# The first cross sequence's query and key projections, its split tile and its score stacks made in the last pair of the self-attention

## The chip, the core and the metric

The kernel runs on one core of one Trainium2 chip. The metric is the device time of one execution in microseconds (us), the median of three runs. The page and the trace of the profile come from one further execution.

## What is computed

A decoder layer on x of 16 sequences x 256 positions x 512 (float32), in three parts, each added to its input:

```python
x = x + attn(layernorm(x), w_q, w_kv, w_dense)      # causal, 16 heads of 128, 4 groups of keys and values
x = x + xattn(layernorm(x), ctx, mask, mask, Wq, bq, Wk, bk, Wv, bv)
x = x + ffn(layernorm(x), ...)                       # 8 experts, 2 chosen per token

# xattn takes the 256 positions as channels and the 512 columns as time; 16 heads of 16 channels
q = einsum('oc,bct->bot', Wq, target) + bq
k = einsum('oc,bcs->bos', Wk, source) + bk
v = einsum('oc,bcs->bos', Wv, source) + bv
dot = einsum('bhdt,bhds->bhts', q, k) / 4            # masked, softmax over s
out = einsum('bhts,bhds->bhdt', softmax(dot), v)
```

Float32 products are made of float32r parts: each operand is split into a high part (a rounded copy, on ScalarE) and a low part (the difference, on VectorE or GpSimd), and three matmuls (high x high, high x low, low x high) make one product.

## The kernel before, in words

The program is a chain of blocks (`nc.Block`). Each block holds one instruction stream for SyncE (SP), GpSimd (POOL), ScalarE (ACT), VectorE (DVE) and TensorE (PE), written out by hand; the order in a stream is the order in the code, and streams meet only at semaphores. At the end of a block all five meet at a barrier, so the next block starts when the last of the five has reached its end.

**The self-attention block** (`attention_phase`) goes over 8 pairs of sequences (512 tokens) twice, once for each half of the heads: `body(t, kind, half)`, with `kind` "plain", "turn", "fresh" or, for the last pair of the second half, "last". A pair has 16 units `u` (a head and a sequence): scores on PE, the row maximum on DVE, the exponential on ACT, the scaling on DVE and POOL, transposes on PE, their high and low parts on ACT and DVE (`pT`), the product with the values into `ps_c`, and its high and low parts (`cT`). From unit 12 on come the `dense` products; the last four of them (`dense(t, 1, n)`) stand after the units, behind `values_product(t, NH - 1)`. In all pairs but the last, the key, value and query projections of the next pair stand among these; in the last pair nothing does. SP loads and stores at fixed places; in the last pair its last commands are four stores of the finished rows (L258), one for each dense sum.

**The preparation of the cross-attention** (`cross_preparation`) hands small steps to these streams: the three cross weights are split in units 1 to 6 (`weight_high` on ACT, `weight_low` on DVE, each for a whole weight: four instructions for k and for q, one for v); `first_stats` on DVE in unit 5; `norm_scale_of_cross` on POOL; `first_normalised`, `first_x_high`, `first_context_high` on ACT in units 8, 10 and 14; `lows_of_cross` (both low parts) on POOL after the last unit.

**The cross-attention block** (`cross_attention_phase`) goes over 16 sequences `b` of 4 quads `q` of 4 turns `k`. A stack holds, for one quad, the split queries and keys and the mask rows. "M" scores (`max_scores`, L1871) give the row maxima (`maximum`, L1687, on DVE), which go through `split_maxima`, a transpose, `negmax_rows` on ACT (L1533) and two DMAs (`stack_negmax`, L1236) into the stack; "E" scores (`exp_scores`, L1882) then go to the exponential on ACT (L1538). The M scores run two quads ahead, so a prologue comes before `body(0, ...)`: the projections `k0, k1, q0, q1, v0, v1` of sequence 0 (`piece`, L1799), their bias and mask on DVE (`raw_tile`, `raw_values`), the split tile (`tile_high_part` on ACT, `tile_low_part` on POOL), 18 stack DMAs (`stack_half`, L1190: 15 on SP, 3 on POOL), the M scores of quads 0 and 1, and, for sequence 1, its load, `normalise(1)`, `norm_scale(1)`, `context_low(1)`, `normalised(1)`, `x_high(1)` and the projection `k0`.

## Time and profile before

| | us |
|---|---|
| runs | 2795.73, 2787.54, 2796.38; median 2795.73 |
| the profiled execution | 2785.0, its span 2783.5, mean granted TensorE clock 0.975 |
| TensorE busy | 2608.0 (94% of the span) |
| VectorE, ScalarE, GpSimd busy | 1865.9, 1456.0, 1000.9 |
| self-attention block | to 1382.2 |
| cross-attention block | from 1382.6; first E scores at 1419.99, last ones at 2300.8 |
| experts | from about 2407 |

A share of busy time over the span says little here, since the change touches one seam in a span of 2783.5 us: the last pair of the self-attention and the 37 us between the barrier and the first E scores. The trace is read there.

### The profile page before, as it was taken

The numbers are of one execution on the slowest core, as the hardware profiler recorded it, in microseconds if no ns is written. First come the engines' busy times: TensorE is split into PE (matmuls) and PEld (weight loads), VectorE is DVE, ScalarE is ACT, GpSimd is POOL, SyncE is SP. The second block draws the span as 40 slices with busy tenths as digits, with TensorE's granted clock in tenths as the row PEclk, the third lists the DMA queues.
The fourth block names the chain that finished last, engine by engine and source line by source line (L and its number), as shares of the span: only waits on it lengthen the run. The fifth ranks groups of instructions, "written<-read, shape, count | busy, mean of one in ns | idle before, by whom it ended". The sixth has DMA issues, their size and how long they took to land. (4 is left out here: it accounts for less than half of the span.)

```text
span 2783.5 us, 51139 instructions
## 1 busy us (share of the span) xinstructions
PE 2608.0 (94%) x15536; PEld 1814.1 (65%) x15537; DVE 1865.9 (67%) x3829; ACT 1456.0 (52%) x2868; POOL 1000.9 (36%) x1194
## 2 busy tenths in 40 slices
PE   7999999999999999999879999999999986399997
PEld 6888888888788888888734444444444323277775
DVE  6556655566544555544588889899888776577665
ACT  4334433344433344333357777777777675355554
POOL 2112211122211122111346656656665647433332
PEclk9999999999999999999989999999999998799998
DMA  4102222013212011102155556555555558655554
GB/s 151 68 8 75 75 75 75 14 61 137 85 50 76 32 60 60 60 30 79 35 115 126 133 131 141 131 137 136 132 127 137 128 152 283 234 105 107 106 106 84
DMA packets 144961, 282.49 MB, mean 101 GB/s; under 512 B 44016, under 2 KB 46960, under 8 KB 139760
## 3 DMA queue, kind: packets, MB, share of 16 engines
q1 hardware_dynamic: 116944, 214.99, 26.5%
q0 software_dynamic: 23664, 58.09, 10.1%
q10 hardware_dynamic: 4272, 8.40, 1.0%
q8 instruction: 43, 0.70, 0.1%
q14 instruction: 38, 0.31, 0.0%
HBM read 147.82 MB, written 81.68 MB: 82 GB/s over the span
## 5 line engine op out<-in xcount | busy, mean ns | idle before, releaser
L1687 DVE TENSOR_REDUCE b_negmax<-b_ps_s 128x2 f32<-128x1024 f32 x512 | 611.5, 1218 | 62.7 <-PE b_ps_s L1871 56.0
L293 POOL TENSOR_SCALAR probs<-probs,rinv 128x256 f32<-128x256 f32 x256 | 241.7, 944 | 1086.3 <-DVE rinv L468 1086.2
L1538 ACT ACTIVATE b_probs<-b_ps_s 128x1024 f32<-128x1024 f32 x512 | 520.1, 1020 | 197.7 <-PE b_ps_s L1882 196.7
L334 ACT ACTIVATE probs<-ps_s,negmax 128x128 f32<-128x128 f32 x256 | 94.1, 367 | 483.2 <-DVE negmax L461 483.2
L1895 PE MATMUL b_ps_o<-b_probs,b_v_stack 128*32 128x256 f32 (+1 forms) x2816 | 297.0, 494 | 0.9 <-ACT b_probs L1538 0.7
L1882 PEld LDWEIGHTS b_ps_s<-b_stack 56*128 56x128 f32 x1024 | 96.3, 184 | 273.2 <-issue 165.1
L1882 PE MATMUL b_ps_s<-b_stack 56*128 56x512 f32 x1024 | 258.3, 501 | 13.4 <-DVE b_negmax L1687 7.4
L1871 PE MATMUL b_ps_s<-b_stack 54*128 54x512 f32 x1024 | 229.7, 445 | 34.0 <-DMA b_stack<-b_split 16.9
L582 PE MATMUL ps_proj<-xT_h,wq_h 128*128 128x512 f32 x512 | 216.6, 423 | 0.0
L2581 POOL DMA_INDIRECT out<-e_y,e_place_int x71 | 119.2, 1678 | 251.7 <-DMA out<-e_y,e_place_int 215.6
L582 PE MATMUL ps_proj<-xT_l,wq_h 128*128 128x512 f32 x512 | 201.4, 393 | 0.0
L582 PE MATMUL ps_proj<-xT_h,wq_l 128*128 128x512 f32 x512 | 200.9, 392 | 0.0
L468 DVE RECIPROCAL rinv<-rowsum 128x2 f32<-128x2 f32 x256 | 42.3, 165 | 218.8 <-ACT probs L336 218.8
L582 PE MATMUL ps_d<-wd_h,cT_h 128*128 128x512 f32 x384 | 158.0, 412 | 1.4 <-DVE cT_l L417 1.4
L582 PE MATMUL ps_s<-kT_h,qT_h 128*128 128x128 f32 (+1 forms) x512 | 156.7, 306 | 0.0
L1871 PEld LDWEIGHTS b_ps_s<-b_stack 54*128 54x128 f32 x1024 | 100.0, 191 | 82.4 <-ACT b_probs L1538 44.5
L582 PE MATMUL ps_d<-wd_h,cT_l 128*128 128x512 f32 x384 | 150.8, 393 | 0.0
L582 PE MATMUL ps_d<-wd_l,cT_h 128*128 128x512 f32 x384 | 149.6, 390 | 0.0
L329 ACT ACTIVATE pT_h<-ps_pT 128x384 fp32r<-128x384 f32 x256 | 127.0, 496 | 30.8 <-PE ps_pT L658 30.8
L582 PE MATMUL ps_s<-kT_l,qT_h 128*128 128x128 f32 (+1 forms) x512 | 142.8, 279 | 0.0
L417 DVE TENSOR_TENSOR pT_l<-ps_pT,pT_h 128x384 fp32r<-128x384 f32 x256 | 140.6, 549 | 3.2 <-ACT pT_h L329 3.2
L582 PE MATMUL ps_s<-kT_h,qT_l 128*128 128x128 f32 (+1 forms) x512 | 142.1, 277 | 0.0
(344 smaller groups left out, 6628.0 us busy)
## 6 DMA issues: line engine op xcount, KB each, us to landing
b_stack<-b_split SPq DMA_DIRECT2D x336, 128.0 KB
e_row<-rows_by_expert SPq DMA_DIRECT2D x71, 258.0 KB, 2.9
b_out_tiles<-row_sum_inverses SPq DMA_DIRECT2D x64, 256.0 KB
x<-acc SPq DMA_DIRECT2D x15, 1024.0 KB, 4.7
x_in<-in_x SPq DMA_DIRECT2D x8, 1024.0 KB, 8.3
normalised_x_split<-xT_h SPq DMA_DIRECT2D x8, 1024.0 KB, 9.9
normalised_x_split<-xT_l SPq DMA_DIRECT2D x8, 1024.0 KB, 11.1
acc<-in_x SPq DMA_DIRECT2D x8, 1024.0 KB, 11.4
```

The lines of the kernel that those rows point to most:

```text
L293: nc.gpsimd.tensor_scalar(probs[:, s, P:3 * P], probs[:, s, P:3 * P], rinv[:, s, 1:2], None, ALU.mult).then_inc(probs_done, 1)
L329: nc.scalar.activation(pT[0][:, u % 4, :], ps_pT[u % 2][:, 0:3 * P], ACT.Copy).then_inc(pT_high, 1)
L334: nc.scalar.activation(probs[:, s, 0:P], ps_s[s][:, 0:P], ACT.Exp, bias=negmax[:, s, 0:1], accum_out=rowsum[:, s, 0:1])
L417: return nc.vector.tensor_tensor(dst, ps, h.bitcast(F32), ALU.subtract)
L468: nc.vector.reciprocal(rinv[:, s, :], rowsum[:, s, :]).then_inc(rinv_done, 1)
L582: ins = nc.tensor.matmul(out, w[a][w_at], m[b][m_at], start=st, stop=en)
L1538: nc.scalar.activation(probs[:, k % 2, p, :, :], ps[:], ACT.Exp, scale=0.25).then_inc(e_done, 1)
L1687: nc.vector.tensor_reduce(negmax[:, k, p, :], ps[:], AX.X, ALU.max, negate=True).then_inc(m_reduced, 1)
L1871: ins = nc.tensor.matmul(ps[:, i, :], stack[rows, quad, 0, p, k * P:(k + 1) * P], stack[rows, quad, 1, p, :], start=True, stop=True)
L1882: ins = nc.tensor.matmul(ps[:, i, :], stack[rows, q, 1, p, k * P:(k + 1) * P], stack[rows, q, 0, p, :], start=True, stop=True)
L1895: ins = nc.tensor.matmul(ps_o[32 * h:32 * h + 32, cols], v_stack[:, k, HQ * q + h, :], probs[:, k % 2, h // 2, h % 2, cols], start=(k == 0 ...
L2581: nc.gpsimd.indirect_dma_start(out, bass.IndirectOffsetOnAxis(place_int[i][:], 0), y[i][:], None, compute_op=ALU.add).then_inc(y_out[i], 16)
```

## The change

In the last pair, `weight_high` and `weight_low` now do one quarter of k or q (or all of v) in each of units 0 to 8 (ACT) and 1 to 9 (DVE). `first_stats` is at units 2 and 3, `norm_scale_of_cross` at unit 5, `first_normalised` at 9 and 10, `first_x_high` at 11, `first_context_high` at 12, the low part of the context in two halves at 13 and 14 (POOL). PE makes the key projections of sequence 0 between the last transposes and the last `values_product`, and the query projections between that and the first of the last four `dense`, in the banks `ps_proj`. DVE, ACT and POOL make the raw tile and the split tile there; SP issues the mask rows, the load of sequence 1 and 15 stack DMAs, and POOL 3, before the block ends. The stack, the raw tiles and the first split tile get addresses that are free there. The cross block's prologue then holds no k or q projection and no tile; the value projections stand behind the third M score, in other banks.

```diff
@@ attention_phase, sync
                 def body(t, kind, half):
-                    if kind == "fresh":
-                        load_weights_of_cross()
...
                     sp.dma_start(acc[:], tokens(rows, t - half * PAIRS)).then_inc(acc_loaded, 16)
+                    if kind == "fresh":
+                        load_weights_of_cross()
...
+                    if kind == "last":
+                        sp.wait_ge(proj_filled, FILLS * (t + 1))
+                        stack_mask_rows()
+                        load_second_sequence()
+                        stack_first_tile()
                     if kind != "last":
@@ gpsimd
-                        if kind == "last" and u == TB + 2:
+                        if kind == "last" and u == TB + 1:
                             norm_scale_of_cross()
+                        if kind == "last" and u in (UNITS - 3, UNITS - 2):
+                            first_context_low(u - (UNITS - 3))
                     if kind == "last":
-                        pool.wait_ge(proj_filled, FILLS * (t + 1))
-                        lows_of_cross()
+                        first_x_low()
+                        first_tile_low()
@@ scalar
-                        if last and u in (1, 3, 5):
-                            weight_high("kqv"[u // 2])
-                        if last and u == 8:
-                            first_normalised()
-                        if last and u == 10:
+                        if last and u < 9:
+                            weight_high("kqv"[u // 4], u % 4)
+                        if last and u in (9, 10):
+                            first_normalised(u - 9)
+                        if last and u == 11:
                             first_x_high()
-                        if last and u == UNITS - 2:
+                        if last and u == UNITS - 4:
                             act.wait_ge(proj_filled, FILLS * (t + 1))
                             first_context_high()
                     probs_transposed(t, UNITS - 1)
+                    if last:
+                        for p in range(2):
+                            first_tile_high("k", p)
...
                     context(t, NH - 1)
+                    if last:
+                        for p in range(2):
+                            first_tile_high("q", p)
@@ vector
-                        if last and u in (2, 4, 6):
-                            weight_low("kqv"[u // 2 - 1])
-                        if last and u == 5:
-                            first_stats()
+                        if last and 1 <= u < 10:
+                            weight_low("kqv"[(u - 1) // 4], (u - 1) % 4)
+                        if last and u in (2, 3):
+                            first_stats(u - 2)
...
+                    if last:
+                        for p in range(2):
+                            first_raw_tile("k", p)
                     c_low_part(t, NH - 1)
+                    if last:
+                        for p in range(2):
+                            first_raw_tile("q", p)
@@ tensor
+                    if last:
+                        pe.wait_ge(proj_low, FILLS * (t + 1))
+                        for p in range(2):
+                            first_projection("k", p)
                     values_product(t, NH - 1)
+                    if last:
+                        for p in range(2):
+                            first_projection("q", p)
@@ cross_preparation
+        def load_second_sequence():
+            sp.wait_ge(ready["xs_low"], 1)
+            sp.wait_ge(ready["cs_low"], 1)
+            sp.dma_start(x_in[:], x1_seq[1].rearrange("(k p) t -> p k t", p=P)).then_inc(xc_loaded, 16)
+            sp.dma_start(c_in[:], context_seq[1].rearrange("(k p) t -> p k t", p=P)).then_inc(xc_loaded, 16)
+
+        def stack_first_tile():
+            sp.wait_ge(ready["tile_low"], 4)
+            for q in range(QUADS - 1):
+                for i in range(2):
+                    if (q, i) != (0, 1):
+                        stack_half(sp, q, i, ready["stacked"][q])
...
+        def first_stats(k):
+            if k == 0:
+                dve.wait_ge(xc_loaded, 32)
+            nc.vector.bn_stats(stats[:, k, :], x_in[:, k, :]).then_inc(ready["stats_done"], 1)
...
+        def first_projection(n, p):
+            src = xs if n == "q" else cs
+            if p == 0:
+                pe.wait_ge(w_low, W_PARTS[n] + 3)
+                pe.wait_ge(ready["xs_low"] if n == "q" else ready["cs_low"], 1)
+            if n == "q":
+                pe.wait_ge(ready["raw_done"], p + 1)
             for k in range(CT):
+                for a, c in ((0, 0), (0, 1), (1, 0)):
+                    ins = nc.tensor.matmul(banks[p], w[n][a][:, k, p * P:(p + 1) * P], src[c][:, k, :],
+                                           start=(k == 0 and a == 0 and c == 0), stop=(k == CT - 1 and a == 1))
+            ins.then_inc(ready["proj_filled"], 1)
@@ cross_attention_phase, gpsimd
-                for name in TILES:
-                    tile_low_part(0, 0, name)
-                pool.wait_ge(tile_low, 4)
-                stack_half(0, 0, 1, nc.gpsimd)
                 nc.gpsimd.memset(x_res, 0.0).then_inc(xres_clear, 1)
-                pool.wait_ge(xres_clear, 1)
-                load_res(0)
+                context_low(1)
                 for q in range(3):
                     values(0, q)
                 norm_scale(1)
-                context_low(1)
+                pool.wait_ge(xres_clear, 1)
+                load_res(0)
                 x_low(1)
@@ scalar
-                for name in TILES:
-                    tile_high_part(0, 0, name)
                 context_high(1)
                 normalised(1)
                 x_high(1)
                 negmax_rows(None, 0, 0)
@@ tensor
-                for name in TILES + VALUES:
-                    pe.wait_ge(w_low, W_PARTS[name[0]])
-                    piece(None, 0, name, 0)
-                pe.wait_ge(raw_done, len(TILES))
-                pe.wait_ge(vbias_done, len(VALUES))
                 for k in range(TBL):
                     for p in range(2):
                         max_scores("prologue", None, -1, 2, k, p)
+                        if (k, p) == (1, 0):
+                            pe.wait_ge(w_low, W_PARTS["v"])
+                            for name in VALUES:
+                                piece(None, 0, name, 0)
```

**SP at the end of the self-attention block.** The instructions of SP from the load of the sums' input (`acc`) to the first ones behind the barrier. Before:

```order
L243 DMA acc<-x 128x4x512 [waits b_x1_stored,a_consts]
L258 DMA x<-acc 128x512 [waits a_d_added] x4
L206 UNCONDITIONAL_BRANCH
L1208 UNCONDITIONAL_BRANCH [waits barrier_Pool_Activation_PE_DVE_SP_release]
L1230 DMA b_stack<-mask_rows_split 8x2048 [waits b_aux_stored]
L1230 DMA b_stack<-mask_rows_split 8x2048 x5
```

And of the changed kernel:

```order
L241 DMA acc<-x 128x4x512 [waits b_x1_stored,a_consts]
L880 DMA p_stack<-mask_rows_split 8x2048 [waits a_proj_filled]
L880 DMA p_stack<-mask_rows_split 8x2048 x5
L885 DMA p_x_in<-x 128x2x512 [waits b_cs_low,b_xs_low]
L886 DMA p_c_in<-in_context 128x2x512
L844 DMA p_stack<-p_split 16x2x1024 [waits b_tile_low]
L844 DMA p_stack<-p_split 16x2x1024 x14
L263 DMA x<-acc 128x512 [waits a_d_added] x4
L206 UNCONDITIONAL_BRANCH
L1304 UNCONDITIONAL_BRANCH [waits barrier_Pool_Activation_PE_DVE_SP_release]
```

23 DMA commands now stand between the load of `acc` and the four stores of the finished rows, and the barrier behind the stores.

**DVE in unit 2 of the last pair**, from the reciprocal of that unit to the row maxima of unit 3. Before:

```order
L468 RECIPROCAL rinv<-rowsum 128x2 [waits a_exp_done]
L470 TENSOR_SCALAR probs<-probs,rinv 128x128 [waits a_rinv_done]
L417 TENSOR_TENSOR pT_l<-ps_pT,pT_h 128x384 [waits a_pT_high]
L954 TENSOR_TENSOR p_wk_l<-p_w_stage,p_wk_h 128x4x32 [waits b_w_high]
L954 TENSOR_TENSOR p_wk_l<-p_w_stage,p_wk_h 128x4x32 x3
L460 TENSOR_REDUCE negmax<-ps_s 128x1 [waits a_s_filled]
```

In the changed kernel:

```order
L481 RECIPROCAL rinv<-rowsum 128x2 [waits a_exp_done]
L483 TENSOR_SCALAR probs<-probs,rinv 128x128 [waits a_rinv_done]
L430 TENSOR_TENSOR pT_l<-ps_pT,pT_h 128x384 [waits a_pT_high]
L1029 TENSOR_TENSOR p_wk_l<-p_w_stage,p_wk_h 128x4x32 [waits b_w_high]
L1037 BN_STATS p_stats<-p_x_in 128x6 [waits b_xc_loaded]
L473 TENSOR_REDUCE negmax<-ps_s 128x1 [waits a_s_filled]
```

One quarter of `wk` is left here (the first stands in unit 1), and the first statistics, which wait for the loads of `x_in` and `c_in`, moved forward from unit 5.

**ACT behind the barrier.** Before:

```order
L1525 ACTIVATE b_split<-b_raw_k 128x512 [waits b_raw_done] x2
L1525 ACTIVATE b_split<-b_raw_q 128x512 [waits b_raw_done] x2
L1501 ACTIVATE p_c_h<-p_c_in 128x1024 [waits b_vbias_done,b_xc_loaded]
L1511 ACTIVATE p_xn<-p_x_in,p_shift,p_rstd 128x512 [waits b_xs_low,b_scale_done]
L1511 ACTIVATE p_xn<-p_x_in,p_shift,p_rstd 128x512
L1516 ACTIVATE p_x_h<-p_xn 128x1024 [waits b_xn_done]
L1533 ACTIVATE b_nm_rows<-b_ps_p 8x512 [waits b_proj_filled]
```

In the changed kernel:

```order
L1580 ACTIVATE p_c_h<-p_c_in 128x1024 [waits b_vbias_done,b_xc_loaded]
L1590 ACTIVATE p_xn<-p_x_in,p_shift,p_rstd 128x512 [waits b_xs_low,b_scale_done]
L1590 ACTIVATE p_xn<-p_x_in,p_shift,p_rstd 128x512
L1595 ACTIVATE p_x_h<-p_xn 128x1024 [waits b_xn_done]
L1612 ACTIVATE b_nm_rows<-b_ps_p 8x512 [waits b_proj_filled]
```

The four instructions of the split tile are gone from here; the row of maxima (`b_nm_rows`) still stands behind the three steps of sequence 1.

**DVE behind the barrier.** Before:

```order
L1677 TENSOR_TENSOR b_v_raw<-b_ps_s,p_bias_v 128x512 [waits b_proj_filled,b_bias_v_loaded]
L1677 TENSOR_TENSOR b_v_raw<-b_ps_s,p_bias_v 128x512 [waits b_proj_filled]
L1656 BN_STATS p_stats<-p_x_in 128x6 [waits b_xc_loaded]
L1656 BN_STATS p_stats<-p_x_in 128x6
L1659 BN_AGGR p_mv<-p_stats 128x2 [waits b_stats_done,b_w_low]
L1659 BN_AGGR p_mv<-p_stats 128x2
L1687 TENSOR_REDUCE b_negmax<-b_ps_s 128x2 [waits b_m_filled] x8
```

In the changed kernel:

```order
L1764 TENSOR_REDUCE b_negmax<-b_ps_s 128x2 [waits b_m_filled] x4
L1754 TENSOR_TENSOR b_v_raw<-b_ps_p,p_bias_v 128x512 [waits b_proj_filled,b_bias_v_loaded]
L1754 TENSOR_TENSOR b_v_raw<-b_ps_o,p_bias_v 128x512 [waits b_proj_filled]
L1764 TENSOR_REDUCE b_negmax<-b_ps_s 128x2 [waits b_m_filled] x2
L1733 BN_STATS p_stats<-p_x_in 128x6 [waits b_xc_loaded]
L1733 BN_STATS p_stats<-p_x_in 128x6
```

Four maxima stand ahead of the raw values now, and six ahead of the statistics of sequence 1.

## Rows read from the trace of the kernel before

**Rows 1.** Window: its length, busy PE, PEld, DVE, ACT, POOL, PE clock, DMA share.

```profile
1408.00:1420.00 12.00, 9.30 (x28) 4.47 (x28) 11.20 (x12) 0.59 (x1) 3.20 (x5) 0.51 0.50 93
```

**Rows 2.** Timeline of PE at the seam: start, duration, line, tiles, idle before.

```profile
1367.18 0.50 PE L582 MATMUL ps_c<-pT_h,v_h 128*128 128x512 f32 x1 [1.17 <-DVE pT_l L417]
...
1369.91 0.50 PE L582 MATMUL ps_d<-wd_h,cT_h 128*128 128x512 f32 x1 [1.41 <-DVE cT_l L417]
...
1382.78 0.47 PE L1799 MATMUL b_ps_p<-p_c_h,p_wk_h 128*128 128x512 f32 x1 [1.69 <-PEq L206]
...
1388.36 0.28 PE L1799 MATMUL b_ps_s<-p_wv_h,p_c_h 128*128 128x256 f32 x1
...
1398.27 1.65 PE L1871 MATMUL b_ps_s<-b_stack 54*128 54x512 f32 x6 [6.91 <-DMA b_stack<-b_split]
...
1417.18 0.79 PE L1799 MATMUL b_ps_p<-p_c_h,p_wk_h 128*128 128x512 f32 x1
...
1419.99 0.50 PE L1882 MATMUL b_ps_s<-b_stack 56*128 56x512 f32 x2
```

**Rows 3.** Timeline of DVE in a plain pair.

```profile
1225.67 0.69 DVE L486 TENSOR_TENSOR acc<-ps_c,acc 128x512 f32<-128x512 f32 x1 [2.03 <-PE ps_c L582]
...
1264.63 0.69 DVE L486 TENSOR_TENSOR acc<-ps_d,acc 128x512 f32<-128x512 f32 x1
```

**Rows 4.** Timeline of DVE in the last pair and behind it.

```profile
1308.35 0.69 DVE L486 TENSOR_TENSOR acc<-ps_c,acc 128x512 f32<-128x512 f32 x1 [2.03 <-PE ps_c L582]
...
1316.16 1.26 DVE L954 TENSOR_TENSOR p_wk_l<-p_w_stage,p_wk_h 128x128 fp32r<-128x128 f32 x4
...
1351.96 0.69 DVE L486 TENSOR_TENSOR acc<-ps_d,acc 128x512 f32<-128x512 f32 x1
...
1381.13 0.69 DVE L486 TENSOR_TENSOR acc<-ps_c,acc 128x512 f32<-128x512 f32 x1 [2.03 <-PE ps_c L582]
...
1390.05 0.69 DVE L1677 TENSOR_TENSOR b_v_raw<-b_ps_s,p_bias_v 128x512 f32<-128x512 f32 x1 [0.73 <-PE b_ps_s L1799]
...
1393.48 1.28 DVE L1656 BATCH_NORM_STATS2 p_stats<-p_x_in 128x6 f32<-128x512 f32 x2 [1.40 <-DMA p_c_in<-in_context]
...
1399.10 9.14 DVE L1687 TENSOR_REDUCE b_negmax<-b_ps_s 128x2 f32<-128x1024 f32 x8 [3.98 <-PE b_ps_s L1871]
1408.27 1.29 DVE L1692 CAST b_nm_split<-b_negmax 128x16 fp32r<-128x16 f32 x1
```

**Rows 5.** Timeline of SP: issues of DMAs (start, time to issue, count).

```profile
1311.91 0.50 SPq L831 DMA_DIRECT2D p_c_in<-in_context  x1
...
1373.69 8.49 SPq L258 DMA_DIRECT2D x<-acc  x4
...
1391.42 6.08 SPq L1190 DMA_DIRECT2D b_stack<-b_split  x9
...
1411.71 1.45 SPq L1236 DMA_DIRECT2D b_stack<-b_nm_rows  x2
```

**Rows 6.** Timeline of POOL.

```profile
1315.63 0.95 POOL L293 TENSOR_SCALAR probs<-probs,rinv 128x256 f32<-128x256 f32 x1 [2.21 <-DVE rinv L468]
...
1397.68 4.99 POOL L1400 TENSOR_SCALAR b_v_stack<-b_v_raw,p_mask_col 128x64 f32<-128x64 f32 x12
...
1404.43 2.35 POOL L1380 TENSOR_TENSOR p_c_l<-p_c_in,p_c_h 128x1024 fp32r<-128x1024 f32 x1
```

**Rows 7.** Timeline of ACT.

```profile
1404.50 1.52 ACT L1511 ACTIVATE p_xn<-p_x_in,p_shift,p_rstd 128x512 f32<-128x512 f32 x2 [9.96 <-POOL p_shift L1376]
1406.05 1.06 ACT L1516 ACTIVATE p_x_h<-p_xn 128x1024 fp32r<-128x1024 f32 x1
1411.06 0.59 ACT L1533 ACTIVATE b_nm_rows<-b_ps_p 8x512 f32<-8x512 f32 x1 [3.95 <-PE b_ps_p L1846]
```

**Rows 8.** DMAs issued between 1309 and 1325: KB each, us to landing.

```profile
p_c_in<-in_context SPq DMA_DIRECT2D x1, 512.0 KB, 5.8
```

**Rows 9.** The stack DMAs (line L1190) of the whole trace.

```profile
L1190 SPq DMA_DIRECT2D b_stack<-b_split x336: 573/597/2775, 1391.4 to 2241.6; - x168
...
DMA to landing us min/median/max: 3.2/3.7/5.8
```

189 lines of the change are left out of this document (102 added, 87 removed).

## The prediction

> **What bounds the kernel at this seam.** I read the timeline of each engine around the change first, then the windows. Behind the barrier TensorE makes the projections of sequence 0 from 1382.78, is done at 1391.36, and sits idle 6.91 us until the stacks land at 1398.27 [rows 2]. From there on VectorE paces: eight maxima take 9.14 us, 1.14 each, and a split of the maxima follows [rows 4]. The sixteenth is followed by the first E scores at 1419.99 [rows 2]. From the barrier (PE at 1382.78) to them are 37.2 us. I take what comes after to be bound as before, so that an earlier start of the E scores is an earlier end.
>
> In the last pair itself VectorE paces too. In a plain pair the time from its last sum (1225.67) to the next pair's first (1264.63) is 38.96 us [rows 3]; in the last pair 43.61 us (1308.35 to 1351.96) [rows 4]. The 4.65 us more are about what the split weights and the statistics cost VectorE: four quarters take 1.26 us, the statistics 1.28, and v's part, 512 columns, about the 0.69 of its neighbours [rows 4]: with k and q 4.5. And the block ends with SP: its last store waits for the sum that starts at 1381.13 and ends at 1381.82 [rows 4], is issued at 1382.18 (1373.69 + 8.49) [rows 5], and PE starts 0.60 later [rows 2].
>
> **The change, part by part.** The sum goes from the end of the block to the first E scores.
>
> *The weight pieces.* The same instructions stand one to a unit in place of four in a row. If VectorE paces, a quarter costs its 0.3 us wherever it stands: 0. The bounds are a gain of 4.65 (all hidden) and the rival below. I take 0, since the extra time of the pair equals the work.
>
> *The first statistics.* They stand in unit 2 now and wait for both loads. The command for `c_in` is issued at 1311.91 [rows 5] and lands 5.8 us later [rows 8], at 1317.7. VectorE would come there at about 1316.75: in the trace of before its quarters start at 1316.16 at the same place of the stream [rows 4], plus two quarters (one of unit 1, one of unit 2). It stands still for 1.0 us, and what stands behind it (the maxima of unit 3, and with them scores, exponentials, transposes) is late by that: **+1.0**. Bounds 0 and 2, as the landing is counted from the issue's start or its end and by the semaphore.
>
> *The projections in the tail.* 24 matmuls of 512 columns took from 1382.78 to 1388.36, 5.58 us [rows 2]. The key half covers TensorE's idle 1.17, the query half its idle 1.41 [rows 2]; their operands are ready, as POOL makes the context's low part in units 13 and 14 and the input's right behind unit 15, in 2.35 us [rows 6], and the query half starts only at about 1369.6. Dense starts **2.45** us later by following the instructions one by one (5.58 less 2.58 is 3.0; the restart behind an idle stretch, 0.1 slower each time, and the finer spacing give back the rest). Bounds 2.4 and 4.
>
> *SP.* The low tile ends some 6 us behind the start of the query projections: the last quarter is filled at 1372.5; VectorE takes 0.7 for 512 columns [rows 4], ACT 0.6 [rows 7], POOL 1.2 (half of 2.35 [rows 6]), and semaphores lie between, so 1375.7, or 1376.7 with the statistics' 1.0. Then 15 stack commands at 0.676 (9 in 6.08 [rows 5]) are 9.8 to 10.1 us: 1386.6. Only then come the four stores, whose sums are all done by then (the last at 1381.82 + 1.0 + 2.45 = 1385.3), at 0.45 each (a load of `c_in` took 0.50 [rows 5]): 1388.4. With the 0.60 to PE the block gives way at **1389.0**, 6.2 later than before, of which 1.0 and 2.45 are above and **2.8** is SP's queue. Bounds 0 (the stores keep pace) and 5 (each command at 1.0).
>
> *The prologue.* Stacks for quad 0 were issued from 1376.7 on and land after 3.2 to 5.8 us [rows 9], long before 1389.0, so the 6.91 us are gone, and the projections' 8.6 too. But a chain that was hidden before has less cover. With S = 1389.0: VectorE starts its maxima at S + 0.8 (1399.10 against 1398.27); the value projections stand in front of the fourth M score, 24 matmuls of 256 columns, 2.8 us (from 1388.36 to the idle at 1391.36 [rows 2]), and cost it 0.7; the fourth maximum ends at S + 6.0, the two raw values (0.69 [rows 4]) at S + 7.3. ACT's high part of the context, 1.06 for 1024 columns [rows 7], waits for them: S + 8.5. POOL's low part, 2.35: S + 10.9; its twelve products for the values, 4.99 [rows 6]: S + 15.9; the scale and shift, 1.8 (its products end at 1402.67 and ACT starts at 1404.50 [rows 6, 7]): S + 17.7. ACT then does 1.52 + 1.06 and only after them the row of maxima, 0.59 [rows 7]: S + 20.9, though TensorE has transposed them by about S + 14. SP takes 1.45 to issue [rows 5]: S + 22.3. Landing: no row shows that DMA's; it lies between 0 and the 5.8 of the stack DMAs [rows 9], and I take 3. The first E scores then start at **S + 25.3 = 1414.3**. VectorE would allow S + 22 (0.8 + 16 x 1.14, 0.7 idle, 1.3 raw values, 1.5 statistics, a split of 0.2 to 1.3 [rows 4], less the last maximum). So the gain to there is 1420.0 - 1414.3 = **5.7 us**; bounds 1 and 9 by the landing and SP.
>
> *The clock.* In the 12 us ahead of the E scores TensorE had 0.51 of its clock, the lower of 1.2 and 2.4 GHz, at 9.30 us busy [rows 1], and it rose as the E scores began, since the projection `k0` from 1417.18 to 1419.99 [rows 2] kept it busy right up to them. Now there is a hole of 1 to 3 us between that projection and the E scores, so the body likely begins at 1.2 GHz for a few us. Such a stretch doubles matmul time (`k0` took 2.81 for its six matmuls, where 5.58 for 24 behind the barrier make 1.40 for six [rows 2]); I take 3 us of it, of which half shows: **-1.5**. Bounds 0 and 3.
>
> Sum: 5.7 - 1.5 = 4.2 us less, of the profiled execution's 2785.0: 2780.8. That execution was 10.7 below the median of the runs (2795.73), and one run of three lay near it. Against the median: **2791.5**.
>
> **The rivals.** A measurement of this kernel tells about 0.3%, 8.4 us, from no change.
>
> *A. Everything is hidden (faster).* If the maxima's rows land in 1 us, SP keeps up (2 back), TensorE enters and stays at 2.4 GHz, and the pieces hide part of their time behind VectorE's waits for each exponential, the gain is 5.7 + 2 + 2 + 1 or more: 11, 2784.7. Against it: VectorE's stream is strictly in order, and a piece behind `pT_l` cannot fill a wait that stands behind the next maxima. Chance 0.18.
>
> *B. SP becomes the bound of the seam (slower).* The median issue of a stack command is 597 ns, but the longest took 2775 [rows 9]. The stores and the barrier stand behind all fifteen. From 1.0 us each on (5 more) the gain is gone; at 1.6 each, 14 us more, the kernel ends 10 later: 2805. For it: the longest ones stand where other transfers were in flight, as the 1 MB load of sequence 1 is here. Against it: nine in a row kept 0.676 [rows 5]. Chance 0.06.
>
> *C. VectorE waits for POOL at each piece (slower than forecast, within 0.3%).* Each piece reads two SBUF tiles while POOL scales probabilities. Here the row shows pieces from 1316.16 to 1317.42 beside POOL's 1315.63 to 1316.58 [rows 4, 6], four in 1.26, with no wait to be seen. The cast at 1408.27 took 1.29 us for 16 columns while POOL subtracted [rows 4], so there is such a wait for another form. Were it so for the pieces, nine times up to 0.4 us would be 3.6 more, 2795.1. Chance 0.10, inside "same".
>
> The Trainium skill, SBUF — State Buffer, "Who interferes with whom", says that a VectorE instruction with two SBUF inputs contends with GpSimd reads and that whoever comes second is blocked until the first has finished. By that rule C would hold; the cast's row agrees with an exclusive wait, the row of the pieces does not.
>
> *D. The block-local cost outweighs (same).* The clock stays at 1.2 GHz from the start of the prologue: the value projections take 5.6 in place of 2.8, everything behind them comes 3 later: 2794.5. Chance 0.2, inside "same".
>
> **How the numbers follow.** The forecast (gain 1 to 8 us) has 0.46, D 0.2, C 0.1, A 0.18, B 0.06. Of these the forecast, C and D are within 0.3%, A faster, B slower; for the spread of the runs (2787.54 to 2796.38) I move 0.04 from same to slower: faster 0.20, same 0.69, slower 0.11. The likeliest case alone spans 2784 to 2795; with A and the runs' lower level, range 2779 to 2799.
>
> **What the changed profile would show.** A DVE idle of 1 us before the first statistics in unit 2; the interval 43.61 at 44.6; dense in the tail 2.45 later against the last add of the units; SP's four stores in one run right behind fifteen stack commands, and the barrier behind them; no wait for a stack in the prologue; ACT's `b_nm_rows` about 4 us or more behind its transposes, and the first E scores waiting for its DMA, 25 us behind the barrier in place of 37; a clock of 0.5 at the start of the body. The prediction is wrong if the interval falls to 39 (pieces hidden), if SP's commands take 1 us or more, or if something in `body(0, ...)` or later that was ready before becomes late (POOL's work of sequence 1 ends only about 1413, 3 us later than before).

## The result, and the profile after

The changed kernel takes 2799.59 us, the median of 12 runs (2795.36 to 2815.62), beside 2791.12 for the kernel before (12 runs, 2781.79 to 2797.81): ratio 1.0041, 95% interval 1.0024 to 1.0058. It is slower by some 11 us by the ratio, 8.5 by the medians; the forecast was 4.2 us less than before. (That forecast, 2791.5, was set against a median of three runs of the kernel before, 2795.73; twelve runs give 2791.12.) Its profiled execution took 2797.36 us, the span 2795.9 against 2783.5.

I laid the two traces side by side at marks that both have:

| mark | before | after | after is later by |
|---|---|---|---|
| GpSimd's first scaling in the "fresh" pair (pair 8, the first of the second half) | 719.42 | 720.12 | 0.70 |
| last sum of the pair ahead of the last one | 1308.35 | 1318.83 | 10.48 |
| first sum of the last pair (interval 43.61, now 44.23) | 1351.96 | 1363.06 | 11.10 |
| last sum of the block | 1381.13 | 1394.67 | 13.54 |
| TensorE behind the barrier | 1382.78 | 1398.97 | 16.19 |
| first E scores | 1419.99 | 1426.47 | 6.48 |
| last E scores | 2300.8 | 2313.84 | 13.04 |
| first product of the experts | 2407.30 | 2420.58 | 13.28 |
| end of the span | 2783.5 | 2795.9 | 12.4 |

From the sum ahead of the last pair to the first E scores ("the seam" below) the changed kernel needs 107.64 us in place of 111.64: 4.0 less. The prediction said 5.7 less up to this mark, and 4.2 with a cost of the clock behind it. But the kernel comes to the seam 10.5 us late, and loses 6.6 more between the first and the last E scores.

**Ahead of the seam.** In the "fresh" pair GpSimd and TensorE, by their timelines; in brackets the idle time before and what ended it:

```profile
720.12 0.95 POOL L298 TENSOR_SCALAR probs<-probs,rinv 128x256 f32<-128x256 f32 x1 [28.01 <-DVE rinv L481]
737.95 0.31 POOL L918 MEMSET p_aux<- 128x256 f32 x1 [16.88 <-DMA p_mask_cut<-in_mask]
738.24 0.93 POOL L298 TENSOR_SCALAR probs<-probs,rinv 128x256 f32<-128x256 f32 x1
...
739.31 0.87 PE L677 MATMUL ps_pT<-ident,probs 128*128 128x128 f32 x3 [9.99 <-POOL probs L298]
```

The same place in the kernel before:

```profile
728.23 0.31 POOL L857 MEMSET p_aux<- 128x256 f32 x1 [7.86 <-DMA p_mask_cut<-in_mask]
728.51 0.93 POOL L293 TENSOR_SCALAR probs<-probs,rinv 128x256 f32<-128x256 f32 x1
...
729.59 0.52 PE L658 MATMUL ps_pT<-ident,probs 128*128 128x128 f32 x3 [0.96 <-POOL probs L293]
```

GpSimd's first step on the mask stands ahead of its second scaling of probabilities and waits for the mask's load. SP's timelines, before and then after, show when that load is issued:

```profile
723.75 0.51 SPq L815 DMA_DIRECT2D p_mask_cut<-in_mask  x1
```

```profile
724.03 0.38 SPq L259 DMA_DIRECT2D x<-acc  x1
724.45 1.67 SPq L214 DMA_DIRECT2D wd_raw<-in_a_wd  x2
729.29 0.37 SPq L241 DMA_DIRECT2D acc<-x  x1
729.70 0.51 SPq L857 DMA_DIRECT2D p_mask_cut<-in_mask  x1
```

Before, the mask was issued first and landed 4.5 us later (723.75 to 728.23), and TensorE waited 0.96 for it. Now it stands behind two loads of 1 MB (`wd_raw`), the wait for a store and a third such load (`acc`), is issued 5.95 later, and lands after 8.25. TensorE waits 9.99, 9.03 more than before; right behind that wait products of 512 columns take 0.63 and 0.78 us in place of 0.39, until about 742.7.

**The seam.** The lines that answer to [rows 4] and [rows 5]; first DVE:

```profile
1318.83 0.69 DVE L499 TENSOR_TENSOR acc<-ps_c,acc 128x512 f32<-128x512 f32 x1 [2.03 <-PE ps_c L601]
...
1324.19 0.38 DVE L1029 TENSOR_TENSOR p_wk_l<-p_w_stage,p_wk_h 128x128 fp32r<-128x128 f32 x1
...
1326.95 0.39 DVE L1029 TENSOR_TENSOR p_wk_l<-p_w_stage,p_wk_h 128x128 fp32r<-128x128 f32 x1
1327.82 0.69 DVE L1037 BATCH_NORM_STATS2 p_stats<-p_x_in 128x6 f32<-128x512 f32 x1 [0.48 <-DMA p_c_in<-in_context]
...
1363.06 0.69 DVE L499 TENSOR_TENSOR acc<-ps_d,acc 128x512 f32<-128x512 f32 x1
...
1386.51 0.69 DVE L499 TENSOR_TENSOR acc<-ps_d,acc 128x512 f32<-128x512 f32 x1 [1.99 <-PE ps_d L601]
...
1394.67 0.69 DVE L499 TENSOR_TENSOR acc<-ps_c,acc 128x512 f32<-128x512 f32 x1 [2.03 <-PE ps_c L601]
```

SP:

```profile
1386.58 9.60 SPq L844 DMA_DIRECT2D p_stack<-p_split  x15
1396.22 2.15 SPq L263 DMA_DIRECT2D x<-acc  x4
...
1422.05 1.39 SPq L1332 DMA_DIRECT2D p_stack<-b_nm_rows  x2
```

PE and ACT up to the first E scores:

```profile
1398.97 1.65 PE L1944 MATMUL b_ps_s<-p_stack 54*128 54x512 f32 x6 [4.34 <-PEq L206]
...
1400.55 0.58 PE L1872 MATMUL b_ps_p<-p_wv_h,p_c_h 128*128 128x256 f32 x1
...
1405.49 0.97 PE L1944 MATMUL b_ps_s<-p_stack 54*128 54x512 f32 x6
...
1415.33 1.01 PE L1919 MATMUL b_ps_p<-p_ident,b_nm_split 128*8 128x128 f32 x4 [3.67 <-DVE b_nm_split L1771]
...
1426.47 0.50 PE L1955 MATMUL b_ps_s<-p_stack 56*128 56x512 f32 x2 [1.05 <-DMA p_stack<-b_nm_rows]
...
1418.89 1.52 ACT L1590 ACTIVATE p_xn<-p_x_in,p_shift,p_rstd 128x512 f32<-128x512 f32 x2 [9.29 <-POOL p_shift L1459]
1420.44 1.06 ACT L1595 ACTIVATE p_x_h<-p_xn 128x1024 fp32r<-128x1024 f32 x1
1421.40 0.57 ACT L1612 ACTIVATE b_nm_rows<-b_ps_p 8x512 f32<-8x512 f32 x1
```

The stores come in one run behind fifteen commands, no stack is waited for in the prologue (the 6.91 of [rows 2] is gone), and the first E scores stand 27.5 us behind the barrier in place of 37.2. The windows show the clock (columns as in [rows 1], the granted clock ahead of the DMA share):

```profile
1399.00:1406.00 7.00, 7.00 (x34) 6.11 (x36) 3.49 (x3) 0.00 (x0) 3.60 (x3) 0.58 0.69 209
1420.00:1426.00 6.00, 4.76 (x12) 2.39 (x10) 5.93 (x8) 1.94 (x3) 5.35 (x8) 0.56 0.74 117
```

The value projections ran mostly at the lower level, 1.2 of 2.4 GHz: from 1400.55 to 1405.49, 4.9 us for what takes 3.0 in [rows 2] (1388.36 to 1391.36). TensorE had been idle for 4.34 us at the barrier, but the length of that wait alone does not decide: in two kernels below the granted clock of the first 7 us was 0.76 behind an idle 4.32, and 0.54 behind an idle 2.59.

**Behind the seam.** In the thirteenth sequence TensorE waits once for a stack; GpSimd, then PE:

```profile
2093.16 1.28 POOL L1463 TENSOR_TENSOR b_split<-p_raw_q,b_split 128x512 fp32r<-128x512 f32 x1 [0.63 <-ACT b_split L1604]
2097.97 1.56 POOL L1287 DMA_DIRECT2D p_stack<-b_split  x3 [3.53 <-issue]
...
2107.04 0.80 PE L1944 MATMUL b_ps_s<-p_stack 54*128 54x512 f32 x2 [6.03 <-DMA p_stack<-b_split]
```

The tile is ready at 2094.44, but GpSimd issues its three stack DMAs only 3.53 later; in other sequences it is 0.62. From this sequence's load of x to the next one's are 60.70 us, in a plain sequence 53.3. "Issue" says that the profile shows nothing that it waited for. The kernel before has one such gap too, but elsewhere, inside the four loads for the residual, and nobody waited for those:

```profile
2049.61 0.51 POOL L1408 DMA_DIRECT2D b_out_tiles<-x  x1 [0.15 <-issue]
2053.23 1.74 POOL L1408 DMA_DIRECT2D b_out_tiles<-x  x3 [3.11 <-issue]
...
2086.77 1.55 POOL L1190 DMA_DIRECT2D b_stack<-b_split  x3 [0.62 <-POOL b_split L1380]
```

The sequence with that gap takes 55.64. One pair of traces does not give its price exactly: in most traces one to four further sequences take 55 to 57 us, at places that change from one trace to the next (in the changed kernel the one from 1705.12, for one: 55.8 us at a mean granted clock of 0.94), and two traces of one and the same kernel (the shorter loop below) have 880.41 and 884.57 us from the first to the last E scores. Over all traces the difference stands: 876.7 to 880.8, mean 879.1, in the three whose gap is not ahead of stacks and whose prologue is the old one, and 878.7 to 894.3, mean 886.6, in the fifteen with the gap ahead of stacks.

### The profile page after: what moved, and what is told of

The parts are those of the page before. It is cut to its first block and busy times, and to the rows that moved or that the text cites. A ratio compares the mean times of both kernels' runs of the same rounds, so it can differ in the third digit from the quotient of the medians.

```text
span 2795.9 us, 51135 instructions
## 1 busy us (share of the span) xinstructions
PE 2609.3 (93%) x15536; PEld 1817.3 (65%) x15537; DVE 1868.7 (67%) x3829; ACT 1457.0 (52%) x2868; POOL 1003.1 (36%) x1195
## 5 line engine op out<-in xcount | busy, mean ns | idle before, releaser
L1955 PEld LDWEIGHTS b_ps_s<-p_stack 56*128 56x128 f32 x1024 | 96.4, 185 | 275.6 <-issue 163.5
L1955 PE MATMUL b_ps_s<-p_stack 56*128 56x512 f32 x1024 | 258.7, 502 | 15.7 <-DVE b_negmax L1764 6.7
L1944 PE MATMUL b_ps_s<-p_stack 54*128 54x512 f32 x1024 | 228.4, 443 | 35.2 <-DVE b_negmax L1764 13.7
L1944 PEld LDWEIGHTS b_ps_s<-p_stack 54*128 54x128 f32 x1024 | 99.5, 190 | 83.0 <-ACT b_probs L1617 46.0
L677 PE MATMUL ps_pT<-ident,probs 128*128 128x128 f32 x768 | 126.7, 274 | 17.6 <-POOL probs L298 17.6
```

The source lines that it names most:

```text
L677: ins = nc.tensor.transpose(ps_pT[s][:, j * P:(j + 1) * P], probs[:, s, j * P:(j + 1) * P], ident[:])
L1944: ins = nc.tensor.matmul(ps[:, i, :], stack[rows, quad, 0, p, k * P:(k + 1) * P], stack[rows, quad, 1, p, :], start=True, stop=True)
L1955: ins = nc.tensor.matmul(ps[:, i, :], stack[rows, q, 1, p, k * P:(k + 1) * P], stack[rows, q, 0, p, :], start=True, stop=True)
```

## Experiments

Three theories stood at the start. The place of the loads costs 10 us and the rest gives 4. Or the lateness is an accident of one execution. Or the seam's edits, or new addresses, cost something later.

**The loads' place alone, with the rest of before.** In the kernel before:

```diff
                 def body(t, kind, half):
-                    if kind == "fresh":
-                        load_weights_of_cross()
...
                     sp.dma_start(acc[:], tokens(rows, t - half * PAIRS)).then_inc(acc_loaded, 16)
+                    if kind == "fresh":
+                        load_weights_of_cross()
```

> The kernel before with one line moved: in the "fresh" pair the 21 loads for the cross-attention (mask, three weights, biases) stand behind the load of the sums' input in place of at the head of the pair. Theory 1 (the loads' place is the loss; GpSimd's first step on the mask stands ahead of its scaling of the probabilities): the mask is issued about 6 us later (729.70 against 723.75 in the two traces) and lands in 8 us in place of 4.5, TensorE waits some 10 us for the probabilities once, and the kernel is 9 to 10 us slower than before, 1.0035. Theory 2 (the lateness in that pair is an accident of one execution): within 2 us of before, with no such wait in its trace. Theory 3 (the change of addresses brings it): the same as theory 2.

2800.76 us beside 2791.12, ratio 1.0037 (1.0021 to 1.0053). Its trace has the one wait, and leaves the seam as it was (111.81):

```profile
737.26 0.31 POOL L857 MEMSET p_aux<- 128x256 f32 x1 [16.84 <-DMA p_mask_cut<-in_mask]
```

And from its table of TensorE's waits (total, times, longest):

```profile
PE ps_pT L658 <- POOL probs L293: 15.5, 17, 10.0
```

The last sum ahead of the last pair comes at 1319.29, 10.9 later than before. So the moved call alone makes the kernel slower.

**The changed kernel with the loads back at the head.**

> The changed kernel with these 21 loads back at the head of the "fresh" pair. Theory 1: the 10 us are gone and the seam alone is left, which the two traces put at 4.0 us less than before (+10.48 at the last sum of the pair ahead, +6.48 at the first E scores): 0.9986 of before, 2787. Theory 2 (the seam or the stacks' new addresses cost something in the sixteen sequences too; from the first E scores to the end the changed kernel lost 5.9 us more): 2 to 6 us slower than before. Theory 3 (the loads' place is no cause): still 8 or more slower.

2793.76 beside 2791.12, 1.0018 (1.0002 to 1.0034). The longest wait for probabilities in that pair is 0.9, the last sum ahead of the last pair at 1307.83, the seam 106.98, 4.7 less than before; and yet the kernel is not faster, but some 5 us slower. Theory 1's 0.9986 missed. The second theory's part on the sixteen sequences holds: 884.4 us from first to last E scores (880.8 before), with a wait of 6.5 for the stack in the thirteenth. The two pieces of this trace give some 2 us more than before; the measured 5 has an interval from 0.6 to 9.5.

**Only the mask's load at the head.**

```diff
+                    if kind == "fresh":
+                        load_mask_cut()
...
         def load_weights_of_cross():
-            sp.dma_start(mask_cut[:], ...).then_inc(mask_loaded, 16)
```

> The changed kernel with only the first of the 21 loads, the mask (0.5 us to issue), at the head of the "fresh" pair; weights and biases stay behind. If the late mask is the whole cause: as with all loads early, within 2 us of it, no wait above 1.5 us of TensorE for the probabilities in that pair. If the weights and biases on the queue cost something of their own (the load of the sums' input was 10 us earlier in the changed kernel, 729.29 against 739.12): a difference of 2 us or more to either side.

2792.97, ratio 1.0012 (0.9997 to 1.0027), no wait above the bound in that pair, the seam 106.72. It agrees with all loads early: the late mask, one command out of 21, was the cost, and no cost of the other twenty is seen.

**Six stack commands on ScalarE's queue.**

```diff
+        def stack_third_quad():
+            act.wait_ge(ready["tile_low"], 4)
+            for i in range(2):
+                stack_half(nc.scalar, QUADS - 2, i, ready["stacked"][QUADS - 2])
```

> As with all loads early, and six of the 15 stack DMAs (those of the third quad) are issued by ScalarE's queue, idle there, in place of SP's. The changed trace shows 15 commands in 9.60 us, four stores in 2.15 behind them, the last at 1398.37, 3.01 behind the end of the last sum (1395.36), and TensorE 0.60 later. If SP's queue sets the end of the block: nine commands end at about 1392.4 on that trace's clock, each store follows its sum, the last is issued 0.5 behind it, and TensorE starts 2.2 to 2.7 us earlier against the last sum; the first E scores 1.5 to 2.5 us earlier, below what 5 rounds tell (the trace must show it). If the six DMAs collide on the other queue or with the loads of sequence 1, the stacks come late: a wait of TensorE for a stack in the prologue of 1 us or more and no gain.

2792.62, ratio 0.9999 (0.9982 to 1.0016). The two queues slowed each other; SP, then ACT:

```profile
1378.31 8.04 SPq L845 DMA_DIRECT2D p_stack<-p_split  x9
1386.39 2.82 SPq L263 DMA_DIRECT2D x<-acc  x4
...
1378.31 5.98 ACTq L845 DMA_DIRECT2D p_stack<-p_split  x6
```

Nine commands at 0.89 each in place of 0.64. From the last sum to TensorE's start it took 3.42 us, where the kernel with all loads early took 4.67: half of what I expected.

**What places GpSimd's gap.** My first theory was a count of its DMAs. Three kernels put idle DMAs of 128 KB into its stream:

```diff
+                for n in range(3):
+                    nc.gpsimd.dma_start(idle[n].rearrange("q d t -> d q t"), rows(x1_seq, 0, n % HQ)).then_inc(idle_stored, 16)
                 nc.gpsimd.memset(x_res, 0.0).then_inc(xres_clear, 1)
```

> As with all loads early, and at the head of the cross-attention block GpSimd issues three more DMAs of 128 KB each (rows of x to a place in memory that nothing reads; no output changes). All four traces with the new prologue show one gap of 3.53 us ("issue") in GpSimd's queue ahead of the stack DMAs of the thirteenth sequence, and TensorE waits 5.9 to 6.8 us for that stack; both traces with the old prologue show the gap three DMAs earlier in GpSimd's order, inside four loads that nobody waits for (3.11 us). The change took three GpSimd DMAs out of this block. Theory 1 (the gap comes after a fixed number of GpSimd DMAs counted from the block's start): it moves back into the loads, no wait for a stack above 1.5 us between the first and the last E scores, that stretch takes 878 to 882 us in place of 884 to 893, and the kernel is 7 to 9 us faster than with the loads early alone: about 2785, 0.998 of before. Theory 2 (the gap comes from the new addresses or from what stands in the stream, not from the count): gap and wait stay where they are, and the time is as before these DMAs or up to 2 us more.

2787.03 beside 2785.12, 1.0001 (0.9983 to 1.0020). The gap did not move (3.52 ahead of the stacks of the thirteenth, TensorE waited 6.4). Theory 1 in its plain form, a fixed number from the block's start, fell.

> The same three DMAs, but issued by GpSimd at the end of the self-attention block, behind its three stack DMAs. If the count starts at the cross block: the gap stays ahead of the stack DMAs and TensorE waits 6 us there. If it runs over the whole program: the gap moves back by three DMAs as in the other kernel, and no such wait is seen.

One run, 2785.72; gap and wait (6.8) stayed, as by the count from the block's start, but that count had fallen with the run beside it.

> The kernel before, its old prologue and old place of the loads, with eight such DMAs at the head of the cross-attention block. By the count, GpSimd's gap moves eight DMAs earlier in its order: from inside the loads of the residual (behind the first of four), past that one, four stores and three stack DMAs, to just ahead of those stack DMAs. Theory 1: a gap of about 3.5 us there, TensorE waits some 6 us for the stack near 2035, and the kernel is 6 to 9 us slower than before (1.0025 to 1.003), plus up to 2 for the eight DMAs themselves beside the first stacks. Theory 2: no wait for a stack of 3 us or more in that stretch, 0 to 2 us slower.

2791.95 beside 2785.12, 1.0025 (1.0009 to 1.0041). The gap left the residual's loads, but went to a later place, not to the earlier one of theory 1: the stacks of the thirteenth sequence, as in the changed kernel. GpSimd's timeline:

```profile
2086.92 1.55 POOL L1190 DMA_DIRECT2D b_stack<-b_split  x3 [3.53 <-issue]
```

TensorE's waits between 2064 and 2128:

```profile
PE b_ps_s L1876 <- DMA b_stack<-b_split: 5.8, 1, 5.8
```

The place was predicted wrongly; the price was right. With a seam 1.2 us longer than before (112.86), some 5 to 6 of its 7 us are left for the gap's new place and the eight DMAs, with nothing else of the change in the kernel. The interval of these 7 us goes from 2.5 to 11.4. This kernel keeps the old addresses, so they are not what the gap at the stacks needs.

> What places GpSimd's gap of 3 us is open: it did not move with three more DMAs at the head of the block or in the block before (134 DMAs of 128 KB stand ahead of it then, 131 in the changed kernel, 128 in the kernel before), but it moved to the stacks of the thirteenth sequence with eight more in the kernel before (139). Here eleven stand there, as many as one sequence issues. If a count decides with some slack (the first group of DMAs behind the 128th or so that meets a condition): gap and wait of 6 us come one sequence earlier, in the twelfth, near 2027. If the place in the program decides (the last turn of the loop over sequences, its twelfth and thirteenth): they stay ahead of the stacks of the thirteenth, near 2080.

> The changed kernel with all loads early and 56 more DMAs of 128 KB by GpSimd, one in every second unit of the first seven pairs. By a count over the program: the gap comes some five sequences earlier, in the seventh or eighth (1760 to 1815), and not in the thirteenth. By the place in the loop: it stays near 2080. A count from the start of the cross-attention block alone gives near 2080 too.

> As with the 56 DMAs, but each of 2 KB. If GpSimd's DMAs are counted, the gap moves as far as with 128 KB each; if their packets or bytes are, it moves by less than one sequence and stays in the thirteenth.

One run each, 2793.65, 2796.06 and 2787.78: the gap stood ahead of the same three stack DMAs each time (3.52, 3.53, 3.53) and TensorE waited 6.4, 6.7 and 6.0. No fixed count of DMAs or of bytes places it.

**A version that should beat both.** The loads early, the statistics back at units 4 and 5, and:

```diff
-                    if (q, i) != (0, 1):
+                    if (q, i) not in ((0, 1), (QUADS - 2, 1)):
                         stack_half(sp, q, i, ready["stacked"][q])
...
+                stack_half(0, QUADS - 2, 1, nc.gpsimd, third_stacked)
                 nc.gpsimd.memset(x_res, 0.0).then_inc(xres_clear, 1)
...
                 context_high(1)
+                negmax_rows(None, 0, 0)
                 normalised(1)
                 x_high(1)
-                negmax_rows(None, 0, 0)
```

> A version that should beat both: the changed kernel with the 21 loads back at the head of the "fresh" pair; the second half of the third quad's stack (three DMAs) issued by GpSimd at the head of the cross-attention block in place of by SP at the end of the self-attention, which shortens SP's queue from 15 to 12 commands and puts three DMAs back into GpSimd's count; ScalarE copies the row of maxima ahead of the two normalisations and the high part of sequence 1; first statistics in units 4 and 5, the scale behind unit 6, as before. Expected: the block ends 2.0 us earlier against its last sum (4.3 to 4.7 becomes 2.5), the pair's interval 43.7 to 44.2 in place of 44.5, the first E scores about 1 us earlier by the row of maxima (TensorE's wait of 1.0 for it gone), the seam 103 to 104.5 us in place of 107 and 111.6; no wait of 6 us in the thirteenth sequence. In all 8 us less than before: 2783, 0.997 (0.9955 to 0.9985). If the count does not place the gap: 2789 to 2791, same as before.

2781.41 beside 2785.12, 0.9986 (0.9969 to 1.0003), so not told apart from no change. The seam is 101.07, 10.6 less than before and better than I expected: the interval 43.52, 2.35 us from the last sum to TensorE's start, and the first E scores 23.6 behind that. About 3 of these us are the clock: in the 7 us behind the barrier it was 1.00 here (0.58 in the changed kernel). Of the runs further down, which have the same prologue, the one with 64 memsets had 0.54 there behind an idle 2.59, and its first E scores came after 26.7; the shorter loop had 1.00 behind an idle 2.55, and 23.8. What sets the level there is open. And the gap stayed at the stacks (3.52, a wait of 6.6), and 6 to 7 us went back.

**No stack DMA on GpSimd in the sequences.**

> The combined version, and GpSimd issues no stack DMA in the sixteen sequences: SP issues the three of the first quad's second half behind the three of its first half, and ScalarE those of the first tile. Then whatever places the gap, only loads and stores of the residual can meet it, for which nobody waits at once. Expected: no wait of TensorE for a stack above 4 us before the last two sequences, the stretch from the first to the last E scores 878 to 881 us in place of 884.9, the seam 101 to 102: 5 us less than the combined version, 9 less than before: 0.997 (0.9955 to 0.9985). If SP's queue (1.9 us more in each sequence) sets the row maxima's DMAs late, each sequence costs up to 0.5 more and the gain is gone: a wait of TensorE for the rows of maxima in each sequence.

2786.56 beside 2788.82, 1.0001 (0.9985 to 1.0017). The trace shows no gap above 0.3 us ahead of a DMA and no wait for a stack above 0.8 before 2150, but a sequence takes 54.1 us in place of 53.3, with a wait of 0.5 to 0.8 for a stack in nearly each, and the stretch is 897.6. The side that I called "SP's queue sets it" came true, on the stacks and not on the rows of maxima. This is the one kernel without the gap, and the one in which GpSimd had issued fewer than 128 DMAs up to 2290 (6096 packets at 48 each are 127; in the others 128 or more stood ahead of the gap). So a lower limit of a count may be part of the condition; no run tests that.

**The code's position and the loop.** With `nc.gpsimd.memset(pads[:, n:n + 1], 0.0)` 64 or 128 times at the head of GpSimd's stream, 32 times in the kernel before, and with the loop one turn shorter:

```diff
-            with eng.Fori(0, (B - 4) // 2) as t:
+            with eng.Fori(0, (B - 6) // 2) as t:
                 body(2 * t + 1, 1, False, False, False)
                 body(2 * t + 2, 0, False, False, False)
+            body(B - 5, 1, False, False, False)
+            body(B - 4, 0, False, False, False)
```

> The combined version with 64 one-column memsets at the head of GpSimd's stream, 1300 us ahead of the loop. Counts of DMAs are ruled out as what places the gap of 3.5 us (it stood ahead of the same stack DMAs with 131 to 187 DMAs ahead of it). If the position of the loop's code in GpSimd's stream places it: the gap is elsewhere than ahead of the stacks of the thirteenth sequence in this kernel or in that with 128 memsets, and where it meets no stack the stretch between first and last E scores is 878 to 881 in place of 885. If the last turn of the loop alone does: same place.

> As with 64 memsets, with 128. If the position of the code places the gap, it stands elsewhere in one of the two; if the loop's last turn does, it is again ahead of the stacks of the thirteenth sequence, 3.5 us, and TensorE waits 6 us.

> The combined version with the loop over sequences one turn (two sequences) shorter, and those two written out behind it on every engine. If the last turn of the loop brings the gap: it moves two sequences earlier, ahead of the stacks of the eleventh, near 1975 in place of 2080. If anything that is counted or timed from the start brings it: it stays near 2080. The written-out sequences may cost waits of their own, up to 3 us each as in the last sequences now.

> The kernel before with 32 one-column memsets at the head of GpSimd's stream and nothing else changed. If GpSimd's gap stood in the harmless place by luck of the code's position: it moves to the stacks of the thirteenth sequence (a gap of 3.53, TensorE waits 6 us) or to another place. If the old prologue's order keeps it there: it stays inside the loads of the residual near 2050, 3.11 us, and no wait for a stack is above 1.5 us before 2190.

One run each: 2775.04, 2786.35, 2775.44 and 2783.99 beside 2789.41. In the first three the gap is again ahead of the stacks of the thirteenth sequence (3.52, 3.52, 3.54; waits 6.0, 6.3, 6.9), in the fourth again inside the residual's loads (3.11). So neither the code's position, by these shifts, nor the loop's last turn places it.

**Timed, and with the stacks kept out of the gap's way once.** In the thirteenth sequence alone SP issues the three DMAs:

```diff
                         stack_half(1 - s, 0, 0, sp)
+                        if static(b) and b == LATE - 1:
+                            stack_half(1 - s, 0, 1, sp, late_stacked)
...
-                        stack_half(1 - s, 0, 1, nc.gpsimd)
+                        if not (static(b) and b == LATE - 1):
+                            stack_half(1 - s, 0, 1, nc.gpsimd)
```

> The same kernel as the combined version with the loop one turn shorter, now timed (one look gave 2775.44 beside 2789.41 for the kernel before, both of which can lie anywhere in a spread of 16 us). Seam 10 us less than before, 6 to 7 given back in the thirteenth sequence: if the loop's length costs and gives nothing, 0.9986 of before as the combined version; if the written-out sequences save the waits at the loop's turn, up to 3 us less, 0.9975.

> The same, and in the thirteenth sequence alone SP issues the three stack DMAs that met GpSimd's gap of 3.5 us in eleven kernels (its queue behind those of the first half). If the gap stays where it is, it now meets a store or load of the residual that nobody waits for at once, or nothing: no wait of TensorE for a stack above 1.5 us in that sequence, which takes 54 to 56 us in place of 61, the stretch from first to last E scores 873 to 877: 6 to 7 us less than the kernel beside it, 0.996 of before (0.9945 to 0.9975), about 2776. If the stall belongs to whoever issues DMAs then, SP shows it and nothing is gained.

The shorter loop: 2781.07 beside 2787.26, 0.9977 (0.9962 to 0.9992). With SP's three DMAs: **2778.01, ratio 0.9960 (0.9943 to 0.9976)**, the fastest of all by its median. The gap is now ahead of GpSimd's stores, and the wait for the stack is 0.8 in place of 6.7; first GpSimd's timeline:

```profile
2101.66 2.13 POOL L1511 DMA_DIRECT2D out<-b_out_tiles  x4 [3.53 <-issue]
```

Then TensorE's waits between 2050 and 2110:

```profile
PE b_ps_s L1962 <- DMA p_stack<-b_split: 0.8, 1, 0.8
```

In time that gave 3 to 5 us, not 6 to 7: from that sequence's load of x to the next one's are 60.5 us in the trace, where I expected 54 to 56, 63.3 in the kernel beside it and 53.3 in a plain one. TensorE waits 2.8 for VectorE's maxima in it, which the kernel beside it does not, and the granted clock falls behind that (0.72 from 2120 to 2129). GpSimd's work behind the gap is still 3.5 late; that this is the cause is argued, not shown. And the stretch from the first to the last E scores is 887.5 in this trace, 884.6 in the one beside it, against an expected 873 to 877. The intervals of these two kernels overlap, so the last edit takes the wait away for certain, and its gain in time is only likely. The median came out where I expected it (2776, 0.996), but not by the steps that I gave. What is clear of noise is that this kernel is faster than the one before.

## Why the prediction was wrong, by its own steps

The time failed for two things that the prediction had no term for.

1. *"I take what comes after to be bound as before", and nothing at all on what comes ahead.* The diff moved `load_weights_of_cross()` in the "fresh" pair. I showed that line in the diff and never costed it: the term stood at nothing, without a reason. The sign was in the trace of before: GpSimd already waited 7.86 us for the mask there, and TensorE 0.96 for GpSimd. The load had no slack, so the whole delay came through: 5.95 later at issue and 3.8 longer in flight, 9.7 us; measured alone 1.0037, 10 us.

2. *"...or something in `body(0, ...)` or later that was ready before becomes late."* I named this as what would make it wrong, and gave it no price and no chance. It came as GpSimd's gap of 3.5 us, ahead of DMAs that TensorE needs: a wait of 6.0, and some 6 to 7 us of the kernel by the stretch between the E scores (6.6 in this pair of traces, 7.5 between the means of fifteen and three) and by the time with eight idle DMAs (7, of which the seam has 1.2).

The sum of the pieces: 10 for the loads, less 4 to 5 at the seam, 6 to 7 for the gap's place are 11 to 13; measured 11.4 by the ratio, 12.4 between the two profiled spans.

The steps at the seam:

- *Pieces, 0:* right. The interval rose by 0.62, of which 0.48 is the wait for `c_in`; nothing was hidden. With the statistics back at units 4 and 5 it is 43.52, as before the change (43.61).
- *First statistics, +1.0:* right in kind: 0.48 here, 0.82 to 1.98 in the eight other kernels with the same order.
- *Dense 2.45 later:* 2.44 (23.45 less 21.01).
- *SP's queue, 2.8, the block giving way 6.2 later:* 2.65 and 5.71 (16.19 less 10.48). Twelve commands in place of fifteen took 2.3 of it away (4.67 to 2.35).
- *First E scores at S + 25.3:* 27.5. The chain is as it was written: ACT's row of maxima last, its end at S + 23.0 (predicted 20.9), SP 1.39, and 3.0 from SP's end to the E scores, as taken. The term that was too small is the value projections: 4.9 us in place of 2.8, at the lower clock. The fourth maximum already ends at S + 8.3 in place of 6.0, and what follows keeps that distance. (The row that the 2.8 names, 1388.36 to 1391.36, has 3.0.)
- *Clock at the body's start, -1.5:* it was low in the prologue already, which is rival D's condition; its 3 were 2.1 here, and 2.9 between two kernels with the same prologue at 1.00 and at 0.54 (23.8 and 26.7). At the body's start it was low too: 0.50 from 1429 to 1432, where the kernel before has 1.00 from 1420 to 1426. But the next load of x stands 7.20 behind the first E scores, 6.89 before, so that cost 0.3 up to there and not 1.5. The forecast had 5.7 at the first E scores and 4.2 with the clock; 4.0 were there, and the two agree only because one cost stood in another term.
- *Rival A:* not in the changed kernel, where SP did not keep up and the clock fell; in the combined version, with SP's queue shortened, the row of maxima earlier and the clock at 1.00, the seam gained 10.6.
- *Rival B:* no: 0.64 a command. With a second queue beside it, 0.89.
- *Rival C:* no. The piece at 1326.95 lay under GpSimd's scaling (1326.41 to 1327.36) and took 0.39, the one at 1324.19 without it 0.38. So the rule weighed there (the Trainium skill, SBUF — State Buffer, "Who interferes with whom") is not seen in these rows.
- *The chances* do not follow from the rivals as listed: with 0.04 moved from same to slower they give faster 0.18, same 0.72, slower 0.10, not 0.20, 0.69 and 0.11. None of them held the two things that decided.

What places the gap is open. It is the same length in all the traces that have it ahead of stacks or stores (3.52 to 3.54), and stands in the thirteenth sequence in every one of these. In the three with GpSimd's old prologue and no idle DMAs it is 3.11 long and one sequence earlier, three loads ahead of those stacks in GpSimd's order. Ruled out are a fixed count of DMAs or bytes, the tested shifts of the code, the loop's last turn and the new addresses. A count together with another condition is not. What of the prologue's order moves it wasn't found.

## What to carry to other kernels

Cost every moved line of a diff, the ones far from its subject first: ask of each moved load which queue waits for it now and with what slack. A wait of 7.86 us on an engine whose next instruction feeds TensorE, with TensorE waiting behind it, says that there is none. A gain at one seam is only as good as what stands behind it: compare the whole run at marks before believing in a local sum, and more than one trace of each kernel where single traces differ by as much as the effect. Where one wait for a DMA appears once in sixteen equal sequences, look at the issuing engine's own queue before blaming the transfer.

## What was not expected of the hardware

- GpSimd's queue stands still once in the cross-attention for 3.1 to 3.5 us ahead of a DMA, with no semaphore that it waited for in the profile. Packets that load instructions were in flight beside it in two of nineteen traces (both of the shorter loop) and in none of the others. In sixteen traces it stands in the same sequence, with 131 to 187 DMAs ahead of it (6288 packets at 48 each in the changed kernel, 131 DMAs). A wait of 5.8 to 6.9 us on TensorE follows where the DMAs behind it are needed. One kernel, whose GpSimd issues no stack DMA in the sequences, has no such gap.
- Two queues that issue at once slow each other: 9 commands in 8.04 us beside 6 in 5.98, where one queue alone issues 15 in 9.60 to 10.18. So 15 took 8.0 in place of some 9.8.
- The mask's 32 KB landed in 4.5 us when it was the first of the loads, with one store of 1 MB issued 0.4 us ahead of it, and in 8.25 behind three loads of 1 MB.
- The granted clock behind the barrier differed between kernels with the same instructions there (0.54 and 1.00, idle 2.59 and 2.55 us ahead), and with it went 2.9 us to the first E scores.
